# An LSTM scan on one core: tanh of the cell written as a sigmoid, placed ahead of the output gate

## The chip, the core and the metric

The kernel runs on one core of one Trainium2 chip. The time is the device time of the core in microseconds, taken as the median of three runs. A profiled execution of the same program gives the trace.

## What is computed

An LSTM over 1,024 steps with batch 2 and width 256 is added to its input; a modulated linear layer then adds to the result.

```python
def step(carry, xw_t):
    prev_h, prev_c = carry
    a = xw_t + prev_h @ Wh
    i = jax.nn.sigmoid(a[:, :Hdim])
    f = jax.nn.sigmoid(a[:, Hdim:2 * Hdim])
    o = jax.nn.sigmoid(a[:, 2 * Hdim:3 * Hdim])
    g = jnp.tanh(a[:, 3 * Hdim:])
    next_c = f * prev_c + i * g
    next_h = o * jnp.tanh(next_c)
    return ((next_h, next_c), next_h)
...
x = x + _L0_cond_ref(x, cond_1024, L0_cond_Wx, L0_cond_Wh, L0_cond_b)
# the second layer: x * (y / 16), times weight, times rsqrt(sum + EPS)
x = x + _L1_cond_ref(x, cond_1024, L1_cond_weight)
```

All arithmetic is in float32.

## The kernel before

The width of 256 stands as two halves of 128 partitions, j = 0 and 1, and everything in a step is done for the one half and then for the other. The scan is a loop of 256 turns (`NBODY`) with four steps in each (`T`, index s), written out by hand for each engine; the order of each engine's instructions is the order of the code, and semaphores join the engines.

**TensorE** makes the sums. A group, `cell(s, j, n, k)`, is the product for output half j, gate n (in, forget, candidate) and input half k of h: four matmuls on 32 columns of weights and 16 columns of `hst` each (`add_h`, L207 to L211). In the trace each float32 matmul is two records. Twelve groups make the three gates of both halves; the six with k = 0 need only the first half of h, the six with k = 1 the second. A step first waits for `h_ready[0]`, does the three groups of j = 0, k = 0 and then one and a half of j = 1, k = 0 (L243 to L248). Then it waits for `h_ready[1]` (L250), does the three groups of j = 0, k = 1, which ends `sums_ready[0]`, the rest of j = 1, and ends `sums_ready[1]`. After that come the four groups of the output gate (`pS`, `osum_ready[j]`), then work that no step waits for at once: the products of x for the next turn (`pX`, L191, 24 matmuls in s = 0 and 1, 16 in s = 2), and in s = 2 and 3 a matmul on zeros (`filler`, `FILL`, L222).

**ScalarE** (L171 to L182) does for each step: sigmoid of the three gates of half 0, the same of half 1 (L176), then for each half the sigmoid of the output gate (L180, from PSUM) and the tanh of the cell (L182, from SBUF), in this order: o0, t0, o1, t1. o waits for `osum_ready[j]`, t for `cell_ready[j]`. The tanh of the candidate g is made from a sigmoid: its weights are doubled, a constant -0.5 stands beside the gates, and so the cell is kept at half its value.

**VectorE** (L335 to L355) makes the cell of each half by two fused multiply-and-sums with their accumulator reads (L340, `junk` and `gates`), and then for each half h = tanh * o into `hst` (L351), which ends `h_ready[j]`. In the last step of a turn it also carries the sums of x into PSUM (`carry_cells`, L322, and `carry_outs`, L326).

**GpSimd** (L130 to L139) waits for both halves of h of a step and adds them to x in place (L137); after the fourth step it copies the x of the turn after next into `xp` (L123), for which TensorE's `pX` work in the next turn's first step waits (`xp_ready`, L266).

After the loop TensorE does the second layer's matmuls (L281, L290), VectorE scales and adds (L368), and SyncE writes out.

Of the kernel before, what the change touches and what calls it, by code (L numbers as in the profile page):

```python
# [4 lines left out]
P = 128  # L5
# [3 lines left out]
ALU = mybir.AluOpType  # L9


def build(nc, xT_in, condT_in, Wx, Wh, bC, w, outT):
    D, B, SEQ = xT_in.shape
    K = D // P
    G = 4
# [10 lines left out]
    WARM = 26  # L26
    FILL = (0, 0, 1, 1)
    NOUT = 512
# [3 lines left out]
    with ctx:  # L32
# [12 lines left out]
        xp = sb("xp", [P, K, ROWS])  # L45
        hst = sb("hst", [P, K, T * WIDE])
        gates = sb("gates", [P, K, B, CELL])
        junk = sb("junk", [P, K, B, G])
        ogate = sb("ogate", [P, K, B])
        zeros = sb("zeros", [P, P])  # L50
        tanhc = sb("tanhc", [P, K, B])
        warmed = sb("warmed", [P, 1])
# [29 lines left out]
        gates_ready = [sem(f"gates_ready{j}") for j in range(K)]  # L82
        bias_doubled = sem("bias_doubled")
        x_carried = [sem(f"x_carried{n}") for n in range(K + 1)]
        cell_ready = [sem(f"cell_ready{j}") for j in range(K)]
        tanh_ready = [sem(f"tanh_ready{j}") for j in range(K)]
        h_ready = [sem(f"h_ready{j}") for j in range(K)]
# [31 lines left out]
        def _(pool):  # L119
# [10 lines left out]
            def bodies(lo, hi, aside=None):  # L130
                with pool.Fori(lo, hi) as it:
                    for s in range(T):
                        for j in range(K):
                            pool.wait_ge(h_ready[j], it * T + (s + 2))
                        at = h_slot((s + 1) % T)
                        now = xh[:, :, :, bass.ds(it * T + s, 1)]
                        pool.tensor_tensor(now, now, hst[:, :, at:at + B].unsqueeze(3), ALU.add).then_inc(xh_ready, 1)  # L137
                    pool.wait_ge(x_summed, it + 2)
                    spread(bass.ds(it * T + 2 * T, T))  # L139
                    if aside is not None:  # L140
                        aside()
# [20 lines left out]
        def _(act):  # L162
# [8 lines left out]
            with act.Fori(0, NBODY) as it:  # L171
                for s in range(T):
                    cols = slice(B * s, B * (s + 1))
                    for j in range(K):
                        act.wait_ge(sums_ready[j], it * T + (s + 1))
                        act.activation(gates[:, j, :, 0:NG].rearrange("p b n -> p n b"), cells[j][:, :, cols],  # L176
                                       ACT.Sigmoid).then_inc(gates_ready[j], 1)
                    for j in range(K):
                        act.wait_ge(osum_ready[j], it * T + (s + 1))
                        act.activation(ogate[:, j, :], outs[j][:, cols], ACT.Sigmoid)  # L180
                        act.wait_ge(cell_ready[j], it * T + (s + 1))
                        act.activation(tanhc[:, j, :], gates[:, j, :, AT_C], ACT.Tanh, scale=2.0).then_inc(tanh_ready[j], 1)  # L182

# [4 lines left out]
        def _(pe):  # L188
# [49 lines left out]

            early, late = range(G // 2), range(G // 2, G)
            with pe.Fori(0, NBODY) as it:  # L240
                for s in range(T):
# [5 lines left out]
                    cell(s, 1, 0, 0)  # L247
                    cell(s, 1, 1, 0, early)  # L248

# [3 lines left out]
                    last.then_inc(sums_ready[0], 1)  # L253
                    cell(s, 1, 1, 0, late)
                    cell(s, 1, 2, 0)
                    for n in range(NG):
# [38 lines left out]
        def _(dve):  # L295
# [20 lines left out]
            dve.wait_ge(wh_loaded, 16)  # L316
            dve.tensor_scalar(wh_sb[:, :, g_cols], wh_sb[:, :, g_cols], 2.0, None, ALU.mult).then_inc(operands_ready, 1)
            for j in range(K):
                dve.tensor_copy(hst[:, j, h_slot(0):h_slot(0) + B], condT[:, j, :]).then_inc(h_ready[j], 1)

# [14 lines left out]
            with dve.Fori(0, NBODY) as it:  # L335
                for s in range(T):
# [11 lines left out]
                    for j in range(K):  # L348
                        dve.wait_ge(tanh_ready[j], it * T + (s + 1))
                        at = h_slot((s + 1) % T)  # L350
                        dve.tensor_tensor(hst[:, j, at:at + B], tanhc[:, j, :], ogate[:, j, :], ALU.mult).then_inc(h_ready[j], 1)  # L351
                        if s == T - 1 and j == 0:
# [45 lines left out]
```

## Time and profile before

| what | us |
|---|---|
| median of three runs | 1866.57 (1865.84 to 1866.58) |
| the profiled execution's own time | 1865.51 |
| its span, first to last instruction | 1863.7 |
| TensorE busy | 1794.8 (96%) |
| VectorE busy | 916.5 (49%) |
| ScalarE busy | 900.9 (48%) |
| GpSimd busy | 259.2 (14%) |

Busy times are modelled for matmuls, and TensorE's busy time counts records that overlap, so 96% isn't TensorE at its peak. Four steps make a turn of the loop; at 1000 us of the span the first records of the steps stand at 1000.73, 1002.50, 1004.26 and 1006.04 us, 1.77 us apart. Times of rows are in microseconds from the start of the span, and two decimals are what the timeline gives.

### The profile page before, as it was taken

How to read it: one execution, taken by the hardware profiler on the slowest of the kernel's cores; microseconds unless marked ns; L12 is line 12 of the kernel's file. 1: busy time of each engine (PE TensorE's matmuls, PEld its weight loads, DVE VectorE, ACT ScalarE, POOL GpSimd, SP SyncE). 2: the span in 40 equal slices, each digit the busy share in tenths (PEclk: the TensorE clock that was granted, in tenths of full speed). 3: DMA queues.
4: the chain of work that ended last, by engine and by line, in shares of the span. 5: the costliest groups of instructions: out<-in, count | busy, mean ns of one | idle time of the engine just before them, and what ended most of it. 6: DMA issues, size and time to landing. Idle time of an engine off the chain costs nothing.

```text
span 1863.7 us, 358217 instructions
## 1 busy us (share of the span) xinstructions
PE 1794.8 (96%) x165116; PEld 1627.1 (87%) x165116; DVE 916.5 (49%) x11034; ACT 900.9 (48%) x6148; POOL 259.2 (14%) x1293
## 2 busy tenths in 40 slices
PE   7999999999999999999999999999999999999998
PEld 6888888888888888888888888888888888888886
DVE  2454544455445544454444544455444544455444
ACT  2444444444444444444444444444444444444443
POOL 0111111111111111111111111111111111111110
PEclk7999999999999999999999999999999999999999
DMA  3000000000000000000000000000000000000001
GB/s 98 0 0 0 0 0 0 0 0 0 0 0 0 0 0 0 0 0 0 0 0 0 0 0 0 0 0 0 0 0 0 0 0 0 0 0 0 0 0 45
DMA packets 4585, 6.69 MB, mean 4 GB/s; under 512 B 1248, under 2 KB 3040, under 8 KB 4576
## 3 DMA queue, kind: packets, MB, share of 16 engines
q1 hardware_dynamic: 3872, 5.51, 0.9%
q10 hardware_dynamic: 704, 1.05, 0.2%
q8 instruction: 7, 0.11, 0.0%
q14 instruction: 2, 0.02, 0.0%
HBM read 4.46 MB, written 2.10 MB: 4 GB/s over the span
## 4 chain that ended last, share of the span: by engine, by line
PE 85%; DVE 10%; ACT 3%; issue 2%; DMA 0%; SPq 0%; POOL 0%; DVEq 0%
PE pG L209 51%; PE pX L191 17%; PE pS L209 12%; DVE junk L340 6%; PE pF L222 3%; ACT gates L176 3%; DVE hst L351 2%; DVE pG L322 1%; PE pX L290 1%; DVE gates L340 0%; DMA xh<-in_xT_dram 0%; PE pS L281 0%; DVE ores L368 0%; SPq L105 0%; ACT tanhc L182 0%
## 5 line engine op out<-in xcount | busy, mean ns | idle before, releaser
L209 PEld LDWEIGHTS pG<-hst,wh_sb 128*32 128x32 f32 x98304 | 981.1, 111 | 219.1 <-DVE hst L351 172.1
L209 PE MATMUL pG<-hst,wh_sb 128*32 128x16 f32 x98304 | 1081.8, 186 | 60.6 <-DVE hst L351 53.4
L340 DVE CUSTOM_DVE_ANT_1 junk<-gates 128x4 f32<-128x4 f32 x4096 | 506.9, 162 | 824.7 <-ACT gates L176 772.5
L176 ACT ACTIVATE gates<-pG 128x6 f32<-128x6 f32 x2048 | 372.5, 182 | 928.7 <-PE pG L209 782.9
L209 PE MATMUL pS<-hst,wh_sb 128*32 128x16 f32 x32768 | 495.5, 185 | 0.0
L191 PE MATMUL pX<-xp,wx_sb 128*32 128x8 f32 x32896 | 459.3, 181 | 2.8 <-issue 1.8
L137 POOL TENSOR_TENSOR xh<-xh,hst 128x4 f32 (+1 forms) x1024 | 208.6, 204 | 1575.4 <-DVE hst L351 1575.4
L182 ACT ACTIVATE tanhc<-gates 128x2 f32<-128x2 f32 x2048 | 410.5, 200 | 13.5
L209 PEld LDWEIGHTS pS<-hst,wh_sb 128*32 128x32 f32 x32768 | 397.9, 108 | 0.0
L191 PEld LDWEIGHTS pX<-xp,wx_sb 128*32 128x32 f32 x32896 | 391.8, 108 | 3.2 <-issue 1.9
L351 DVE TENSOR_TENSOR hst<-tanhc,ogate 128x2 f32<-128x2 f32 x2048 | 329.7, 161 | 100.4 <-ACT tanhc L182 0.2
L340 DVE DVE_READ_ACCUMULATOR2_ANT gates<- 128x1 f32 x4096 | 339.1, 83 | 0.0
L180 ACT ACTIVATE ogate<-pS 128x2 f32<-128x2 f32 x2048 | 338.9, 170 | 0.3
L222 PE MATMUL pF<-zeros,picks 128*32 128x128 f32 x1076 | 214.0, 285 | 0.0
L322 DVE TENSOR_TENSOR pG<-pX,bias_col 128x24 f32<-128x24 f32 x514 | 95.0, 185 | 1.1 <-PE pX L191 1.1
L222 PEld LDWEIGHTS pF<-zeros,picks 128*32 128x32 f32 x1076 | 77.3, 109 | 0.6
L123 POOL COPY xp<-xh 128x16 f32 (+1 forms) x258 | 51.7, 200 | 10.5 <-DMA xh<-in_xT_dram 9.0
L326 DVE TENSOR_TENSOR pS<-pX,bias_o 128x16 f32<-128x16 f32 x257 | 45.2, 176 | 0.0
L290 PE MATMUL pX<-xh,wmod 128*128 128x512 f32 x32 | 14.0, 595 | 0.0
L290 PEld LDWEIGHTS pX<-xh,wmod 128*128 128x128 f32 x32 | 6.0, 190 | 7.2 <-issue 6.9
L368 DVE SCALAR_TENSOR_TENSOR ores<-pX,demod,xh 128x512 f32<-128x512 f32 x8 | 6.0, 750 | 8.0 <-PE pX L290 8.0
L306 DVE TENSOR_SCALAR yscale<-condT 128x4 f32<-128x4 f32 x1 | 0.2, 169 | 7.5 <-DMA condT<-in_condT_dram 7.5
(30 smaller groups left out, 13.9 us busy)
## 6 DMA issues: line engine op xcount, KB each, us to landing
outT_dram<-ores SPq DMA_DIRECT2D x8, 256.0 KB, 2.5
xh<-in_xT_dram SPq DMA_DIRECT2D x6, 320.0 KB
wh_sb<-in_Wh_dram ACTq DMA_DIRECT2D x1, 1024.0 KB, 8.0
wx_sb<-in_Wx_dram SPq DMA_DIRECT2D x1, 1024.0 KB, 7.4
w_sb<-in_w_dram SPq DMA_DIRECT2D x1, 256.0 KB, 6.9
xh<-in_xT_dram SPq DMA_DIRECT2D x2, 64.0 KB, 7.9
condT<-in_condT_dram ACTq DMA_DIRECT2D x1, 2.0 KB, 7.7
bias_col<-in_bC_dram ACTq DMA_DIRECT2D x1, 3.0 KB, 7.4
```

The source lines that it names most:

```text
L123: pool.tensor_copy(xp[:, :, :].rearrange("p k (t b) -> p k b t", b=B), xh[:, :, :, t]).then_inc(xp_ready, 1)
L137: pool.tensor_tensor(now, now, hst[:, :, at:at + B].unsqueeze(3), ALU.add).then_inc(xh_ready, 1)
L176: act.activation(gates[:, j, :, 0:NG].rearrange("p b n -> p n b"), cells[j][:, :, cols], ACT.Sigmoid).then_inc(gates_ready[j], 1)
L180: act.activation(ogate[:, j, :], outs[j][:, cols], ACT.Sigmoid)
L182: act.activation(tanhc[:, j, :], gates[:, j, :, AT_C], ACT.Tanh, scale=2.0).then_inc(tanh_ready[j], 1)
L191: last = pe.matmul(to[c * Q:(c + 1) * Q, :], tile(wx_sb[:, k, :], c, j, g), xp[:, k, :], start=(k == 0), stop=(k == K - 1), skip_group_che ...
L209: last = pe.matmul(to[c * Q:(c + 1) * Q, :], tile(wh_sb[:, k, :], c, j, g), hst[:, k, WIDE * t:WIDE * (t + 1)], start=False, stop=True, sk ...
L222: pe.matmul(pF[0:Q, 0:P], picks[:, :], zeros[:, :], start=start, stop=True, skip_group_check=True)
L322: dve.tensor_tensor(cells[j][:, :, 0:ROWS], xcells[j], bias_col[:, j, :].unsqueeze(2).broadcast_to([P, NG, ROWS]), ALU.add).then_inc(x_car ...
L326: dve.tensor_tensor(pS[:, :, 0:ROWS], xouts, bias_o[:, :].unsqueeze(2).broadcast_to([P, K, ROWS]), ALU.add).then_inc(x_carried[K], 1)
L340: cell = dve.tensor_tensor_reduce(out=junk[:, j, b, :], in0=gates[:, j, b, AT_I:AT_F + 1].unsqueeze(2).broadcast_to([P, 2, 2]), in1=gates[ ...
L351: dve.tensor_tensor(hst[:, j, at:at + B], tanhc[:, j, :], ogate[:, j, :], ALU.mult).then_inc(h_ready[j], 1)
```

## The change

The tanh of the cell becomes a sigmoid of four times the halved cell, `sigc` (tanh(c) = 2 sigmoid(2c) - 1). VectorE's h becomes (sigc - 0.5) * o, which is half of h. The weights `wh_sb` are doubled for it (the candidate's times four in all), and the first h is halved. On ScalarE the order in each step becomes t0, o0, t1, o1, and h of a half waits for its o (`factors_ready[j]`). GpSimd doubles the halved h into a new buffer, `whole`, waits for that and adds it to x: two instructions where there was one. TensorE does one group of j = 1, k = 0 ahead of the wait for the second half of h in place of one and a half, and the matmul on zeros of the fourth step is gone.

```diff
-    FILL = (0, 0, 1, 1)
+    FILL = (0, 0, 1, 0)
...
-                        pool.tensor_tensor(now, now, hst[:, :, at:at + B].unsqueeze(3), ALU.add).then_inc(xh_ready, 1)
+                        pool.tensor_tensor(whole[:, s, :, :], hst[:, :, at:at + B], hst[:, :, at:at + B], ALU.add).then_inc(whole_ready, 1)
+                        pool.wait_ge(whole_ready, it * T + (s + 1))
+                        pool.tensor_tensor(now, now, whole[:, s, :, :].unsqueeze(3), ALU.add).then_inc(xh_ready, 1)
...
                     for j in range(K):
+                        act.wait_ge(cell_ready[j], it * T + (s + 1))
+                        act.activation(sigc[:, j, :], gates[:, j, :, AT_C], ACT.Sigmoid, scale=4.0)
                         act.wait_ge(osum_ready[j], it * T + (s + 1))
-                        act.activation(ogate[:, j, :], outs[j][:, cols], ACT.Sigmoid)
-                        act.wait_ge(cell_ready[j], it * T + (s + 1))
-                        act.activation(tanhc[:, j, :], gates[:, j, :, AT_C], ACT.Tanh, scale=2.0).then_inc(tanh_ready[j], 1)
+                        act.activation(ogate[:, j, :], outs[j][:, cols], ACT.Sigmoid).then_inc(factors_ready[j], 1)
...
-            early, late = range(G // 2), range(G // 2, G)
...
                     cell(s, 1, 0, 0)
-                    cell(s, 1, 1, 0, early)
 
                     pe.wait_ge(h_ready[1], it * T + (s + 1))
                     for n in range(NG):
                         last = cell(s, 0, n, 1)
                     last.then_inc(sums_ready[0], 1)
-                    cell(s, 1, 1, 0, late)
-                    cell(s, 1, 2, 0)
+                    for n in range(1, NG):
+                        cell(s, 1, n, 0)
...
-            dve.tensor_scalar(wh_sb[:, :, g_cols], wh_sb[:, :, g_cols], 2.0, None, ALU.mult).then_inc(operands_ready, 1)
+            ifo_cols = slice(0, (O_ + 1) * D)
+            dve.tensor_scalar(wh_sb[:, :, ifo_cols], wh_sb[:, :, ifo_cols], 2.0, None, ALU.mult)
+            dve.tensor_scalar(wh_sb[:, :, g_cols], wh_sb[:, :, g_cols], 4.0, None, ALU.mult).then_inc(operands_ready, 1)
...
-                        dve.tensor_tensor(hst[:, j, at:at + B], tanhc[:, j, :], ogate[:, j, :], ALU.mult).then_inc(h_ready[j], 1)
+                        dve.scalar_tensor_tensor(out=hst[:, j, at:at + B], in0=sigc[:, j, :], scalar=-0.5, in1=ogate[:, j, :],
+                                                 op0=ALU.add, op1=ALU.mult).then_inc(h_ready[j], 1)
```

On ScalarE, in each step, the rows before the change (the numbers behind the names are the halves):

```order
L176 ACTIVATE gates<-pG 128x3x2 [waits sums_ready0]
L176 ACTIVATE gates<-pG 128x3x2 [waits sums_ready1]
L180 ACTIVATE ogate<-pS 128x2 [waits osum_ready0]
L182 ACTIVATE tanhc<-gates 128x2 [waits cell_ready0]
L180 ACTIVATE ogate<-pS 128x2 [waits osum_ready1]
L182 ACTIVATE tanhc<-gates 128x2 [waits cell_ready1]
```

And with it:

```order
L179 ACTIVATE gates<-pG 128x3x2 [waits sums_ready0]
L179 ACTIVATE gates<-pG 128x3x2 [waits sums_ready1]
L183 ACTIVATE sigc<-gates 128x2 [waits cell_ready0]
L185 ACTIVATE ogate<-pS 128x2 [waits osum_ready0]
L183 ACTIVATE sigc<-gates 128x2 [waits cell_ready1]
L185 ACTIVATE ogate<-pS 128x2 [waits osum_ready1]
```

The output gate's sigmoid moved from ahead of the cell's function to behind it, in both halves.

On TensorE, in the third step of a turn (s = 2), the rows before:

```order
L209 MATMUL pG<-hst,wh_sb 32x16 [waits h_ready0]
L209 MATMUL pG<-hst,wh_sb 32x16 x17
L209 MATMUL pG<-hst,wh_sb 32x16 [waits h_ready1]
L209 MATMUL pG<-hst,wh_sb 32x16 x29
L209 MATMUL pS<-hst,wh_sb 32x16 x16
```

And with the change:

```order
L212 MATMUL pG<-hst,wh_sb 32x16 [waits h_ready0]
L212 MATMUL pG<-hst,wh_sb 32x16 x15
L212 MATMUL pG<-hst,wh_sb 32x16 [waits h_ready1]
L212 MATMUL pG<-hst,wh_sb 32x16 x31
L212 MATMUL pS<-hst,wh_sb 32x16 x16
```

Two matmuls moved from ahead of the wait for the second half of h to behind it: 16 ahead and 32 behind, where there were 18 and 30.

## Rows read from the trace of the kernel before

**Rows 1.** The page: busy time by engine, and the chain that ended last

```profile
PE 1794.8 (96%) x165116; PEld 1627.1 (87%) x165116; DVE 916.5 (49%) x11034; ACT 900.9 (48%) x6148; POOL 259.2 (14%) x1293
...
PE 85%; DVE 10%; ACT 3%; issue 2%; DMA 0%; SPq 0%; POOL 0%; DVEq 0%
```

**Rows 2.** View of waits: who waited for whom, us, times, longest

```profile
PEld pG L209 <- DVE hst L351: 172.1, 513, 0.5
```

**Rows 3.** Timeline, weight loads of one step: start, length, engine, line, operation

```profile
1002.50 0.93 PEld L209 LDWEIGHTS pG<-hst,wh_sb 128*32 128x32 f32 x95
...
1003.62 0.41 PEld L191 LDWEIGHTS pX<-xp,wx_sb 128*32 128x32 f32 x32
...
1004.26 0.44 PEld L209 LDWEIGHTS pG<-hst,wh_sb 128*32 128x32 f32 x40 [0.20 <-DVE hst L351]
```

**Rows 4.** Timeline, ScalarE in the same step; last row: the second L176

```profile
1003.27 0.51 ACT L176 ACTIVATE gates<-pG 128x6 f32<-128x6 f32 x2 [0.74 <-PE pG L209]
1003.75 0.17 ACT L180 ACTIVATE ogate<-pS 128x2 f32<-128x2 f32 x1
1003.82 0.20 ACT L182 ACTIVATE tanhc<-gates 128x2 f32<-128x2 f32 x1
1003.92 0.17 ACT L180 ACTIVATE ogate<-pS 128x2 f32<-128x2 f32 x1
1004.10 0.20 ACT L182 ACTIVATE tanhc<-gates 128x2 f32<-128x2 f32 x1
...
1003.60 0.18 ACT L176 ACTIVATE gates<-pG 128x6 f32<-128x6 f32 x1
```

**Rows 5.** Timeline, VectorE in the same step

```profile
1003.66 0.08 DVE L340 DVE_READ_ACCUMULATOR2_ANT gates<- 128x1 f32 x1
...
1003.98 0.08 DVE L340 DVE_READ_ACCUMULATOR2_ANT gates<- 128x1 f32 x1
1004.05 0.16 DVE L351 TENSOR_TENSOR hst<-tanhc,ogate 128x2 f32<-128x2 f32 x1
...
1004.34 0.16 DVE L351 TENSOR_TENSOR hst<-tanhc,ogate 128x2 f32<-128x2 f32 x1
```

**Rows 6.** Busy by stretch, instructions on hst: matmuls, then loads, counts in brackets

```profile
1004.26:1004.50 0.24, 0.23 (x28) 0.23 (x32) 0.16 (x1) 0.00 (x0) 1.00 0.00 0
```

**Rows 7.** Groups by line and shape: total, mean ns, idle before

```profile
L351 DVE TENSOR_TENSOR hst<-tanhc,ogate 128x2 f32<-128x2 f32 x2048 | 329.7, 161 | 100.4 <-ACT tanhc L182 0.2
...
L169 ACT ACTIVATE warmed<-zeros 128x1 f32<-128x1 f32 x1 | 0.2, 203 | 0.0
...
L306 DVE TENSOR_SCALAR yscale<-condT 128x4 f32<-128x4 f32 x1 | 0.2, 169 | 7.5 <-DMA condT<-in_condT_dram 7.5
```

**Rows 8.** Timeline, GpSimd after the fourth step of a turn

```profile
1006.50 0.20 POOL L137 TENSOR_TENSOR xh<-xh,hst 128x4 f32 x1 [1.57 <-DVE hst L351]
1006.68 0.20 POOL L123 COPY xp<-xh 128x16 f32 x1
```

**Rows 9.** Timeline, weight loads of the step that follows

```profile
1006.04 0.94 PEld L209 LDWEIGHTS pG<-hst,wh_sb 128*32 128x32 f32 x95 [0.48 <-DVE hst L351]
...
1007.19 0.54 PEld L191 LDWEIGHTS pX<-xp,wx_sb 128*32 128x32 f32 x48
```

**Rows 10.** Timeline, all engines before the loop

```profile
10.00 0.42 DVE L317 TENSOR_SCALAR wh_sb<-wh_sb 128x512 f32<-128x512 f32 x1
...
11.67 0.28 DVE L322 TENSOR_TENSOR pG<-pX,bias_col 128x24 f32<-128x24 f32 x2 [1.10 <-PE pX L191]
```

**Rows 11.** Busy time by stretch, all engines, with the granted clock

```profile
core 0: us, PE busy (x) PEld busy (x) DVE busy (x) ACT busy (x) POOL busy (x), PEclk, DMA share, GB/s
12.20:30.70 18.50, 10.62 (x644) 9.67 (x644) 3.29 (x41) 3.41 (x24) 0.61 (x3) 0.50 0.02 5
...
33.00:52.00 19.00, 18.58 (x1722) 17.01 (x1716) 8.93 (x107) 8.75 (x60) 2.61 (x13) 1.00 0.38 117
1000.00:1007.09 7.09, 6.88 (x668) 6.26 (x658) 3.55 (x44) 3.51 (x24) 0.99 (x5) 1.00 0.00 0
```

More of the change, by code:

```diff
@@ L46, in build @@
         hst = sb("hst", [P, K, T * WIDE])
+        whole = sb("whole", [P, T, K, B])
         gates = sb("gates", [P, K, B, CELL])
@@ L50, in build @@
         zeros = sb("zeros", [P, P])
-        tanhc = sb("tanhc", [P, K, B])
+        sigc = sb("sigc", [P, K, B])
         warmed = sb("warmed", [P, 1])
@@ L82, in build @@
         gates_ready = [sem(f"gates_ready{j}") for j in range(K)]
-        bias_doubled = sem("bias_doubled")
+        bias_doubled, whole_ready = sem("bias_doubled"), sem("whole_ready")
         x_carried = [sem(f"x_carried{n}") for n in range(K + 1)]
         cell_ready = [sem(f"cell_ready{j}") for j in range(K)]
-        tanh_ready = [sem(f"tanh_ready{j}") for j in range(K)]
+        factors_ready = [sem(f"factors_ready{j}") for j in range(K)]
         h_ready = [sem(f"h_ready{j}") for j in range(K)]
@@ L316, in _ @@
             dve.wait_ge(wh_loaded, 16)
-            dve.tensor_scalar(wh_sb[:, :, g_cols], wh_sb[:, :, g_cols], 2.0, None, ALU.mult).then_inc(operands_ready, 1)
+            ifo_cols = slice(0, (O_ + 1) * D)
+            dve.tensor_scalar(wh_sb[:, :, ifo_cols], wh_sb[:, :, ifo_cols], 2.0, None, ALU.mult)
+            dve.tensor_scalar(wh_sb[:, :, g_cols], wh_sb[:, :, g_cols], 4.0, None, ALU.mult).then_inc(operands_ready, 1)
             for j in range(K):
-                dve.tensor_copy(hst[:, j, h_slot(0):h_slot(0) + B], condT[:, j, :]).then_inc(h_ready[j], 1)
+                dve.tensor_scalar(hst[:, j, h_slot(0):h_slot(0) + B], condT[:, j, :], 0.5, None, ALU.mult).then_inc(h_ready[j], 1)
             def carry_cells(j):
@@ L348, in _ @@
                     for j in range(K):
-                        dve.wait_ge(tanh_ready[j], it * T + (s + 1))
+                        dve.wait_ge(factors_ready[j], it * T + (s + 1))
                         at = h_slot((s + 1) % T)
-                        dve.tensor_tensor(hst[:, j, at:at + B], tanhc[:, j, :], ogate[:, j, :], ALU.mult).then_inc(h_ready[j], 1)
+                        dve.scalar_tensor_tensor(out=hst[:, j, at:at + B], in0=sigc[:, j, :], scalar=-0.5, in1=ogate[:, j, :],
+                                                 op0=ALU.add, op1=ALU.mult).then_inc(h_ready[j], 1)
                         if s == T - 1 and j == 0:
```

## The prediction

> **What bounds the kernel now.** I read the page first. TensorE is busy 96% of the span, but the chain that ended last also has 10% on VectorE and 3% on ScalarE [rows 1]: TensorE is not alone in setting the pace. The view of waits says the same: the weight loads of the next step waited for VectorE's h 513 times, 172 us in all [rows 2]. So I went to one step in the timeline, the third of a turn. Its weight loads start at 1002.50 and the next step's at 1004.26 [rows 3], 1.77 us apart (rounding aside), and 1,024 steps of 1.77 us are 1,812 of the span's 1863.7 us. All that follows is about that 1.77.
>
> Each step has two loops, one through each half of h. The first half ends at 4.05 + 0.16 = 1004.21 [rows 5], and the loads begin at 1004.26 [rows 3]: TensorE stood waiting and started 0.05 later. So the first half sets the step. The second half ends at 4.34 + 0.16 = 1004.50 [rows 5]; with the same 0.05 TensorE may use it from 1004.55. Does it come in time? 95 loads start within 0.93 less the last one's own 0.11, so 0.0087 us apart [rows 3]; the four and a half groups ahead of the wait are 18 matmuls or 36 records, 0.31 us, and end at 1004.57. The second half is early by about 0.03 us. That is the whole slack, and three edits draw on it.
>
> **The second half's loop, before.** From one end of the second h to the next: 0.05 to TensorE's restart. From there to ScalarE's second gates: the records behind the wait start at 1002.50 + 0.31 = 1002.81, the second L176 at 1003.60 [rows 4], so 0.79. From that to the end of the second cell at 3.98 + 0.08 = 1004.06 [rows 5]: 0.46. To the tanh at 1004.10: 0.04; the tanh: 0.20 [rows 4]. To the product at 1004.34: 0.04; the product: 0.16 [rows 5]. Sum 1.74, which is the 1.77 less the slack of 0.03.
>
> **Four groups, not four and a half.** Two matmuls, 4 records, move behind the wait: 4 x 0.0087 = +0.035 in this loop. For the first half it is a gain: its sums can end 0.035 sooner, if the second h is there.
>
> **The output gate behind the cell's function.** Before, the second half's o had been done long ahead (1003.92 to 1004.09) while the cell was still being made, and only the tanh lay on the path. Now h waits for o, and o stands in ScalarE's queue behind a function that itself waits for the cell. Nothing hides it. How soon may o start behind the other? Two pairs in the rows: o to tanh 3.75 to 3.82, 0.07; tanh to o 3.82 to 3.92, 0.10 [rows 4]. The second has the new order, and I take 0.10. Then the new piece is 0.10 + 0.17 for o, 0.27 in place of 0.20: +0.07. Bounds: with 0.07 it is +0.04. The function itself costs the same: a sigmoid read from SBUF took 203 ns, near the tanh's 0.20 [rows 7], and only its distance to o counts.
>
> The Trainium skill (ScalarE: Activation LUTs, What ACT_TABLE_LOAD costs) says that back-to-back ACTIVATEs overlap by about 93 ns. By it o would start 0.20 - 0.09 = 0.11 behind, and this estimate would add 10 us to the result below; the trace's pairs are a little closer, and the sum goes by them.
>
> **VectorE's product.** The new form has a constant ahead of the product. No row has it in this size; the product takes 161 ns, an operation with a constant on four elements 169 [rows 7]. A gain has no ground: it does one operation more on the same operands. Between 0 and +0.01; I take +0.005.
>
> **TensorE after a real stop.** Now TensorE will stand at the second wait, and resume with its queue full. In the first 0.24 us after a stop 32 loads start but 28 matmuls [rows 6]: 0.0075 and 0.0086 apart, against 0.0087 on average. Over the first 32 records that is between 0 and -0.04; I take -0.02.
>
> **The sum.** 1.74 + 0.035 + 0.07 + 0.005 - 0.02 = 1.83 us for the second half's loop. It is over 1.77, so the slack is gone and this loop becomes the pace: TensorE reaches the wait 32 x 0.0087 = 0.28 after a step's start and the second h comes about 0.08 later, in every step. The first half's own loop would be shorter: its tanh had waited for o (1003.82, where the cell was ready at 3.66 + 0.08 = 1003.74 and 0.04 more is the usual start [rows 4, 5]), so 1.77 - 0.035 - 0.04 + 0.07 = 1.765. It can't run by itself, since its sums are ended behind the same wait. 0.06 us x 1,024 = +61 us on the profiled execution's 1865.51; the median of the runs lies 1 us above it, so 1866.57 + 61 = 1928.
>
> **What lies beside.** GpSimd: two instructions and a wait in place of one. Alone it waits for nothing critical, except in a turn's first step, where its copy of x releases `pX`. Before: the second h ends 2.00 after the fourth step's start [rows 5], at 1006.26; GpSimd adds from 6.50 and its copy ends at 6.68 + 0.20 = 1006.88 [rows 8], 0.31 before `pX` starts at 1007.19 [rows 9]. New: the added instruction costs its 0.20 and a wait for its own result, between 0 and the 0.24 that GpSimd took from the h to its start: +0.20 to +0.44, and the second h comes 0.08 later in the step, as `pX` does. So the copy is late by 0.13 at most. `pX` is the last work of that step; its loads take 0.54 and end at 1007.73, 0.08 before the next at 1007.81 (1006.04 + 1.77) [rows 9], and the longer step adds 0.06 to that. In the worst case nothing is left, and 0 is taken; a wait longer by 0.1 would cost 256 x 0.1 = 26 us.
>
> The matmul on zeros of the fourth step: TensorE stood still afterwards anyway, so it is worth nothing by itself. SyncE's queue isn't touched. Before the loop the scaling of `wh_sb` takes 2,048 in place of 512 elements in each partition: at most 3 x 0.42 = 1.26 us more, where VectorE stood idle 1.10 until 11.67 [rows 10], so 0 to 0.2 us; I take 0. After the loop one more GpSimd instruction, hidden by the first matmuls: 0.
>
> **Rivals.** (A) No loss, or a gain: the two functions go through ScalarE almost side by side, both being of one kind now. The second half's loop is 1.83 with 0.10 between their starts; with 0.04 it is 1.77 and nothing changes, which is the point from which it decides, and with 0.02 it is 1.75: 20 us less, 1846. For it: before, the pairs were of two kinds, a sigmoid and a tanh, and no row shows two sigmoids at that distance. Against: both orders of the mixed pair are at 0.07 and 0.10, and at 0.07 the result is still 1.80, or 1897. Chance 0.07.
>
> (B) GpSimd's copy holds `pX` and through it the next step, as worked out: 1928 + 26 = 1954. For it: 0.24 from h to start shows how slow its waits are. Against: it needs all of the worst case and more. Chance 0.08.
>
> (C) The granted clock falls. Between 12.2 and 30.7 us it was at 0.50, the 1.2 GHz level, with 35 load records a us and steps of some 4.6 us; from 33 us on it was at 1.00 with 90 a us, and 93 in the turn at 1000 us [rows 11]. The new turn has 2 load records less in 7.32 us in place of 7.09, so 90 a us again. If it fell all the same, each 20 steps at that pace would cost 57 us: over 1985. Chance 0.04.
>
> **How the numbers follow.** The forecast (a step of 1.79 to 1.86) gets 0.81. Its bounds: with o at 0.07 and the full 0.04 gained after a stop 1.78, which is 1877; without that gain, with 0.01 for the product, 1.855, which is 1954. I give 1888 to 1966, which takes in (B) and leaves out (A), (C) and the last corner of the lower bounds. A measurement of this kernel can tell 0.2%, 4 us. Faster by more than that: 0.04, slower: 0.92, the same: 0.04.
>
> **What would show it.** In the profile after, the steps lie 1.83 apart; within a step TensorE's loads break after 32 records for about 0.08 us, and the view of waits has TensorE waiting for h twice a step, so over 1,000 times more often. On ScalarE o starts 0.10 behind the cell's function and the product 0.04 behind o's end. If the loads don't break, (A) holds; if `pX` waits for `xp`, (B); if PEclk has a digit under 9 after the first slice, (C). I am wrong if o starts closer than 0.04 to the function ahead of it.

## The result, and the profile after the change

The changed kernel takes 1921.65 us (median of 4 runs, 1920.77 to 1922.18), the kernel before beside it 1866.21 us: a ratio of 1.0298, 95% interval 1.0285 to 1.0311. It is 55.4 us slower; 1928 was predicted, with 1888 to 1966 as the range. The profiled execution took 1921.88 us, its span is 1920.1.

The page after, busy time by engine and the chain that ended last, as in [rows 1]:

```profile
PE 1787.3 (93%) x164604; PEld 1662.8 (87%) x164604; DVE 926.6 (48%) x11035; ACT 885.9 (46%) x6148; POOL 459.7 (24%) x2317
...
PE 84%; DVE 10%; ACT 3%; issue 2%; DMA 0%; SPq 0%; POOL 0%; ACTq 0%; DVEq 0%
```

The chain has hardly changed its shares: it still goes through TensorE for the most part, and the page alone wouldn't say where the time went. The timeline of one step does. The weight loads of the third step of a turn and of the one behind it, as in [rows 3]:

```profile
1004.25 1.01 PEld L212 LDWEIGHTS pG<-hst,wh_sb 128*32 128x32 f32 x95
...
1006.08 0.23 PEld L212 LDWEIGHTS pG<-hst,wh_sb 128*32 128x32 f32 x17 [0.18 <-DVE hst L354]
```

The steps lie 1.83 us apart, where it was 1.77 [rows 3]. The same 95 loads take 1.01 from first start to last end, where it was 0.93: something stands in the middle of them. The view by stretch counts the loads in the first 0.24 and the first 0.35 us of that step (columns: stretch, its length, busy time of the loads and their count, granted clock, DMA):

```profile
1004.25:1004.49 0.24, 0.24 (x32) 1.00 0.00 0
1004.25:1004.60 0.35, 0.34 (x32) 1.00 0.00 0
```

And for the same 0.35 us from a step's start in the kernel before:

```profile
1004.26:1004.61 0.35, 0.34 (x41) 1.00 0.00 0
```

After the change, 32 loads have started by 0.24 us, the 16 matmuls ahead of the wait, and not one more by 0.35. Before, TensorE went on without a break. The missing loads are those behind the wait for the second half of h. ScalarE in that step, as in [rows 4]:

```profile
1005.06 0.18 ACT L179 ACTIVATE gates<-pG 128x6 f32<-128x6 f32 x1 [0.70 <-PE pG L212]
1005.42 0.18 ACT L179 ACTIVATE gates<-pG 128x6 f32<-128x6 f32 x1 [0.18 <-PE pG L212]
1005.56 0.20 ACT L183 ACTIVATE sigc<-gates 128x2 f32<-128x2 f32 x1
1005.67 0.15 ACT L185 ACTIVATE ogate<-pS 128x2 f32<-128x2 f32 x1
1005.92 0.20 ACT L183 ACTIVATE sigc<-gates 128x2 f32<-128x2 f32 x1
1006.03 0.15 ACT L185 ACTIVATE ogate<-pS 128x2 f32<-128x2 f32 x1
```

And VectorE, as in [rows 5], from the h of the step before to the second h of this one:

```profile
1004.39 0.16 DVE L354 SCALAR_TENSOR_TENSOR hst<-sigc,ogate 128x2 f32<-128x2 f32 x1 [0.20 <-ACT ogate L185]
...
1005.81 0.08 DVE L343 DVE_READ_ACCUMULATOR2_ANT gates<- 128x1 f32 x1
1005.86 0.16 DVE L354 SCALAR_TENSOR_TENSOR hst<-sigc,ogate 128x2 f32<-128x2 f32 x1
1006.22 0.16 DVE L354 SCALAR_TENSOR_TENSOR hst<-sigc,ogate 128x2 f32<-128x2 f32 x1 [0.20 <-ACT ogate L185]
```

The second cell ends at 1005.89, its sigmoid starts at 1005.92, the gate at 1006.03 and ends at 1006.18, and only then, at 1006.22, comes the second h. It ends at 1006.38, 1.83 after the one before (1004.39 + 0.16 = 1004.55). So the loop through the second half goes round in 1.83 us, and TensorE stands at its wait in nearly every step.

The costs by group, as in [rows 7]:

```profile
L183 ACT ACTIVATE sigc<-gates 128x2 f32<-128x2 f32 x2048 | 418.4, 204 | 89.9 <-DVE gates L343 2.5
...
L354 DVE SCALAR_TENSOR_TENSOR hst<-sigc,ogate 128x2 f32<-128x2 f32 x2048 | 328.8, 161 | 169.9 <-ACT ogate L185 143.4
...
L185 ACT ACTIVATE ogate<-pS 128x2 f32<-128x2 f32 x2048 | 314.5, 154 | 0.1
```

The cell's function is 204 ns as a sigmoid and the new product 161 ns, what the plain one took: neither has a price. The gate itself takes 154 ns. VectorE's idle time ahead of the product grew from 100.4 [rows 7] to 169.9 us, and 143.4 us of it is put down to the gate; the view names a releaser for the longer gaps alone, so the 0.2 us of [rows 7] doesn't mean that VectorE hardly waited for ScalarE before.

### The profile page after: what moved, and what is told of

Read it like the earlier page. It is cut to its first block, busy times and chain, and to the rows that moved or that the text cites. A ratio compares the mean times of both kernels' runs of the same rounds, so it can differ in the third digit from the quotient of the medians.

```text
span 1920.1 us, 358468 instructions
## 1 busy us (share of the span) xinstructions
PE 1787.3 (93%) x164604; PEld 1662.8 (87%) x164604; DVE 926.6 (48%) x11035; ACT 885.9 (46%) x6148; POOL 459.7 (24%) x2317
## 4 chain that ended last, share of the span: by engine, by line
PE 84%; DVE 10%; ACT 3%; issue 2%; DMA 0%; SPq 0%; POOL 0%; ACTq 0%; DVEq 0%
PE pG L212 52%; PE pX L194 17%; PE pS L212 11%; DVE junk L343 7%; PE pF L225 3%; ACT gates L179 3%; DVE hst L354 2%; DVE pG L325 1%; PE pX L291 1%; DVE gates L343 0%; DMA xh<-in_xT_dram 0%; ACT sigc L183 0%; PE pS L282 0%; DVE ores L372 0%; SPq L106 0%
## 5 line engine op out<-in xcount | busy, mean ns | idle before, releaser
L212 PE MATMUL pG<-hst,wh_sb 128*32 128x16 f32 x98304 | 1142.6, 186 | 123.8 <-DVE hst L354 115.1
L212 PEld LDWEIGHTS pG<-hst,wh_sb 128*32 128x32 f32 x98304 | 1036.7, 111 | 239.4 <-DVE hst L354 186.3
L138 POOL TENSOR_TENSOR whole<-hst 128x4 f32<-128x4 f32 x1024 | 203.7, 199 | 1250.6 <-DVE hst L354 1250.6
L212 PE MATMUL pS<-hst,wh_sb 128*32 128x16 f32 x32768 | 479.8, 185 | 0.0
L183 ACT ACTIVATE sigc<-gates 128x2 f32<-128x2 f32 x2048 | 418.4, 204 | 89.9 <-DVE gates L343 2.5
L354 DVE SCALAR_TENSOR_TENSOR hst<-sigc,ogate 128x2 f32<-128x2 f32 x2048 | 328.8, 161 | 169.9 <-ACT ogate L185 143.4
L185 ACT ACTIVATE ogate<-pS 128x2 f32<-128x2 f32 x2048 | 314.5, 154 | 0.1
L140 POOL TENSOR_TENSOR xh<-xh,whole 128x4 f32 (+1 forms) x1024 | 205.2, 200 | 181.1 <-POOL whole L138 179.2
L225 PE MATMUL pF<-zeros,picks 128*32 128x128 f32 x564 | 110.6, 286 | 0.0
L225 PEld LDWEIGHTS pF<-zeros,picks 128*32 128x32 f32 x564 | 41.7, 110 | 0.4
```

Of the source, the lines that this page charges most:

```text
L138: pool.tensor_tensor(whole[:, s, :, :], hst[:, :, at:at + B], hst[:, :, at:at + B], ALU.add).then_inc(whole_ready, 1)
L140: pool.tensor_tensor(now, now, whole[:, s, :, :].unsqueeze(3), ALU.add).then_inc(xh_ready, 1)
L183: act.activation(sigc[:, j, :], gates[:, j, :, AT_C], ACT.Sigmoid, scale=4.0)
L212: last = pe.matmul(to[c * Q:(c + 1) * Q, :], tile(wh_sb[:, k, :], c, j, g), hst[:, k, WIDE * t:WIDE * (t + 1)], start=False, stop=True, sk ...
L225: pe.matmul(pF[0:Q, 0:P], picks[:, :], zeros[:, :], start=start, stop=True, skip_group_check=True)
L354: dve.scalar_tensor_tensor(out=hst[:, j, at:at + B], in0=sigc[:, j, :], scalar=-0.5, in1=ogate[:, j, :], op0=ALU.add, op1=ALU.mult).then_i ...
```

## The experiments

The theory: a step has two loops, one through each half of h, and the change made the second half's the longer one, by the output gate's 0.06 us behind the cell's function and by the 0.035 us of two more matmuls behind the wait. The rivals: GpSimd's two instructions, the sigmoid form, and the missing matmul on zeros.

The times, with the ratio to runs of the kernel before made beside them (1865.94, 1866.46 and 1865.99 us):

| run | what it is | us | ratio to before, 95% interval |
|---|---|---|---|
| a_o_first | changed, ScalarE's order put back | 1863.28 | 0.9975 to 0.9994 |
| a_18_ahead | changed, 18 matmuls ahead of the wait | 1898.01 | 1.0157 to 1.0191 |
| a_20_ahead | changed, 20 ahead | 1899.19 | 1.0164 to 1.0198 |
| a_14_ahead | changed, 14 ahead | 1954.99 | 1.0462 to 1.0497 |
| a_pool_once | changed, one GpSimd instruction; it leaves out the doubling, so its output has half of h in it | 1920.94 | 1.0277 to 1.0311 |
| a_fill | changed, matmul on zeros put back | 1923.31 | 1.0289 to 1.0323 |
| b_o_behind | before, gate behind the tanh | 1913.90 | 1.0240 to 1.0274 |
| b_16_ahead | before, 16 ahead | 1863.07 | 0.9973 to 0.9992 |
| b_form | before, with the sigmoid form alone | 1868.13 | 1.0004 to 1.0022 |
| b_o_behind_nofill | b_o_behind, no matmul on zeros in the fourth step | 1893.95 | 1.0136 to 1.0167 |
| b_best17 | before, another order and 17 ahead | 1883.03 | 1.0076 to 1.0106 |
| b_best17_nofill | the same, no matmul on zeros there | 1882.44 | 1.0074 to 1.0102 |

**a_o_first: the order of ScalarE put back**

```diff
-                    for j in range(K):
-                        act.wait_ge(cell_ready[j], it * T + (s + 1))
-                        act.activation(sigc[:, j, :], gates[:, j, :, AT_C], ACT.Sigmoid, scale=4.0)
-                        act.wait_ge(osum_ready[j], it * T + (s + 1))
-                        act.activation(ogate[:, j, :], outs[j][:, cols], ACT.Sigmoid).then_inc(factors_ready[j], 1)
+                    act.wait_ge(osum_ready[0], it * T + (s + 1))
+                    act.activation(ogate[:, 0, :], outs[0][:, cols], ACT.Sigmoid)
+                    act.wait_ge(cell_ready[0], it * T + (s + 1))
+                    act.activation(sigc[:, 0, :], gates[:, 0, :, AT_C], ACT.Sigmoid, scale=4.0).then_inc(factors_ready[0], 1)
+                    act.wait_ge(osum_ready[1], it * T + (s + 1))
+                    act.activation(ogate[:, 1, :], outs[1][:, cols], ACT.Sigmoid)
+                    act.wait_ge(cell_ready[1], it * T + (s + 1))
+                    act.activation(sigc[:, 1, :], gates[:, 1, :, AT_C], ACT.Sigmoid, scale=4.0).then_inc(factors_ready[1], 1)
```

> The changed kernel with ScalarE's order put back: output gate, cell's function, for each half. Theory (the second half's loop through h is the pace, and the output gate behind the cell's function is most of what it gained): the loop falls by the 0.26 us from the function's start to the gate's end less the function's 0.20, so by 0.06 from 1.83 to 1.77, where the first half's loop, whose function again waits for the gate, takes over: 1860 to 1867 us. Rival (GpSimd's doubling, the sigmoid form or the missing matmul on zeros cost the time): 1915 or more.

Measured 1863.28. Everything else of the change is still in it, and it is 58 us faster than the changed kernel and 2.7 faster than the one before. So without the new order nothing is left of the loss. That doesn't make the order all of it: the next two runs and a_18_ahead below show what the two matmuls take beside it.

**b_16_ahead, b_o_behind: each part of the change alone, in the kernel before**

b_16_ahead is the change's edit on TensorE:

```diff
-                    cell(s, 1, 1, 0, early)
...
-                    cell(s, 1, 1, 0, late)
+                    cell(s, 1, 1, 0, range(0, G))
                     cell(s, 1, 2, 0)
```

> The kernel before, with nothing changed but 16 matmuls ahead of the second h in place of 18. Theory: the second half's loop goes from 1.745 by 0.035 to 1.78 less up to 0.02, the first half's stays at 1.77, since its tanh waits for the output gate's sums, which are not moved: 0 to 8 us more, 1866 to 1874. Rival (the two parts of the change cost by themselves what they cost together): 20 us more.

Measured 1863.07: no cost, a gain of 3.4 us, on the other side of what I had expected. Its steps are 1.771 us in the trace where the kernel before has 1.769, so the gain is not in them; the section on the turn's start below has what it may be. So the two matmuls cost nothing by themselves, while the second half's loop has slack; with the new order they cost 24 us (1898.01 with 18 ahead, 1921.65 with 16).

b_o_behind is the change's order on ScalarE, with tanh:

```diff
-                    for j in range(K):
-                        act.wait_ge(osum_ready[j], it * T + (s + 1))
-                        act.activation(ogate[:, j, :], outs[j][:, cols], ACT.Sigmoid)
-                        act.wait_ge(cell_ready[j], it * T + (s + 1))
-                        act.activation(tanhc[:, j, :], gates[:, j, :, AT_C], ACT.Tanh, scale=2.0).then_inc(tanh_ready[j], 1)
+                    act.wait_ge(cell_ready[0], it * T + (s + 1))
+                    act.activation(tanhc[:, 0, :], gates[:, 0, :, AT_C], ACT.Tanh, scale=2.0)
+                    act.wait_ge(osum_ready[0], it * T + (s + 1))
+                    act.activation(ogate[:, 0, :], outs[0][:, cols], ACT.Sigmoid).then_inc(tanh_ready[0], 1)
+                    act.wait_ge(cell_ready[1], it * T + (s + 1))
+                    act.activation(tanhc[:, 1, :], gates[:, 1, :, AT_C], ACT.Tanh, scale=2.0)
+                    act.wait_ge(osum_ready[1], it * T + (s + 1))
+                    act.activation(ogate[:, 1, :], outs[1][:, cols], ACT.Sigmoid).then_inc(tanh_ready[1], 1)
```

> The kernel before, with nothing changed but ScalarE's order: tanh, output gate, for each half, and h waits for the gate. Theory: the second half's loop goes from 1.745 by 0.06 to 1.80, its slack of 0.025 is spent and 0.035 are left, less what TensorE gains after a stop: 20 to 36 us more, 1886 to 1902, as much as the changed kernel with 18 matmuls ahead. Rival (a sigmoid behind a sigmoid costs more than behind a tanh, or the rest of the change has a price): clearly below that kernel.

Measured 1913.90, 12 us over the range. Three of its four steps are 1.79 to 1.80 us, as the theory has it. The turn's first step is 1.92, with a stop of TensorE near its start that the theory doesn't have (below). In the other three steps the theory holds: with the gate in the same place and a tanh ahead of it, the gate starts 0.11 behind and the steps are those of a_18_ahead.

**b_form: what is left of the change**

The edits of a_o_first, and with them:

```diff
-    FILL = (0, 0, 1, 0)
+    FILL = (0, 0, 1, 1)
...
                     cell(s, 1, 0, 0)
+                    cell(s, 1, 1, 0, range(2))
...
-                    for n in range(1, NG):
-                        cell(s, 1, n, 0)
+                    cell(s, 1, 1, 0, range(2, G))
+                    cell(s, 1, 2, 0)
```

> The changed kernel with ScalarE's order, the 18 matmuls ahead and the matmul on zeros of the kernel before: what is left of the change is the sigmoid form, h halved, the product with a constant and GpSimd's two instructions. Theory: the form costs nothing, since a sigmoid takes the tanh's 204 ns and the new product the old one's 161: 1864 to 1869 us. Rival (the form has a price of its own): 5 us more or above.

Measured 1868.13, 2.1 us above the kernel beside it and within what was expected. By the interval, the sigmoid form, the halved h and GpSimd's doubling cost 1 to 4 us together.

**a_14_ahead, a_18_ahead, a_20_ahead: how many matmuls stand ahead of the wait**

a_18_ahead:

```diff
                     cell(s, 1, 0, 0)
+                    cell(s, 1, 1, 0, range(2))
...
-                    for n in range(1, NG):
-                        cell(s, 1, n, 0)
+                    cell(s, 1, 1, 0, range(2, G))
+                    cell(s, 1, 2, 0)
```

a_20_ahead:

```diff
                     cell(s, 1, 0, 0)
+                    cell(s, 1, 1, 0, range(4))
...
-                    for n in range(1, NG):
-                        cell(s, 1, n, 0)
+                    cell(s, 1, 2, 0)
```

a_14_ahead:

```diff
-                    cell(s, 1, 0, 0)
+                    cell(s, 1, 0, 0, range(2))
...
                     last.then_inc(sums_ready[0], 1)
+                    cell(s, 1, 0, 0, range(2, G))
```

> The changed kernel with three and a half groups (14 matmuls) ahead of the second h. Theory: two more matmuls in the second half's loop, 0.035 us a step, 36 us more: 1957. Rival (the wait is hidden or TensorE makes it up after a stop): under 1940.

> The changed kernel with four and a half groups (18 matmuls) ahead of the second h, as before the change. Theory: 4 records of 0.0087 us leave the second half's loop, 1.83 becomes 1.795, and the first half's own loop (0.31 to the wait and 1.47 from there) is at 1.78 just under it: 36 us less, 1886. Rival (the wait for the second h is not what paces): within 5 us of 1921.6.

> The changed kernel with five groups (20 matmuls) ahead of the second h. Theory of two loops: the second half's falls to 1.76, but the first half's sums now end later, 0.345 us to the wait and 1.47 from there, 1.815: 1907 us, so slower than with 18 though faster than with 16. Rival (only the second half's loop counts): a further 36 us less, 1850.

With 14, 16, 18 and 20 ahead: 1954.99, 1921.65, 1898.01, 1899.19. The first difference is 33 us for two matmuls, 0.033 us a step, against 0.035 forecast. From 18 to 20 nothing more is gained, though two more matmuls leave the second half's loop: the other loop has taken over. It is a little shorter than the expectation for 20 had it, 1.804 in place of 1.815 us, and so the time lies 8 us under the forecast of 1907. The starts of the weight loads in a turn of a_20_ahead show it:

```profile
1044.89 0.91 PEld L212 LDWEIGHTS pG<-hst,wh_sb 128*32 128x32 f32 x96 [0.60 <-DVE hst L354]
...
1046.69 0.91 PEld L212 LDWEIGHTS pG<-hst,wh_sb 128*32 128x32 f32 x96
...
1048.50 0.91 PEld L212 LDWEIGHTS pG<-hst,wh_sb 128*32 128x32 f32 x96
```

The loads take 0.91, with no stop among them, and the steps are 1.80 and 1.81 apart: TensorE waits for the first h alone. In a_18_ahead the steps should be 1.795:

```profile
1045.40 0.94 PEld L212 LDWEIGHTS pG<-hst,wh_sb 128*32 128x32 f32 x95 [0.57 <-DVE hst L355]
...
1047.23 0.93 PEld L212 LDWEIGHTS pG<-hst,wh_sb 128*32 128x32 f32 x95
...
1049.02 0.94 PEld L212 LDWEIGHTS pG<-hst,wh_sb 128*32 128x32 f32 x95
...
1050.82 0.94 PEld L212 LDWEIGHTS pG<-hst,wh_sb 128*32 128x32 f32 x95 [0.21 <-DVE hst L355]
```

Three are (1.79, 1.80, 1.79), and the first of the turn is 1.83. The 12 us by which it missed the forecast are for the most part that 0.035 to 0.04 in each of 256 turns, 9 to 10 us. The next section has what it probably is.

**a_pool_once, a_fill: the rivals taken away**

a_pool_once:

```diff
-                        pool.tensor_tensor(whole[:, s, :, :], hst[:, :, at:at + B], hst[:, :, at:at + B], ALU.add).then_inc(whole_ready, 1)
-                        pool.wait_ge(whole_ready, it * T + (s + 1))
-                        pool.tensor_tensor(now, now, whole[:, s, :, :].unsqueeze(3), ALU.add).then_inc(xh_ready, 1)
+                        pool.tensor_tensor(now, now, hst[:, :, at:at + B].unsqueeze(3), ALU.add).then_inc(xh_ready, 1)
```

a_fill:

```diff
-    FILL = (0, 0, 1, 0)
+    FILL = (0, 0, 1, 1)
```

> The changed kernel with one GpSimd instruction a step, as before the change: it adds the halved h to x, so the doubling is left out and the output holds half of h. In the profile after the change the first cell instruction of a turn's first step takes 198 ns in place of 165 while GpSimd copies x, and that step is 1.863 us long, but the next is 1.796. Theory: the delay is in the first half alone, which is not the pace, and is given back a step later: 1919 to 1922 us, with four steps of 1.83. Rival (GpSimd's second instruction costs part of the 55 us): 8 us less or more.

> The changed kernel with the matmul on zeros in the fourth step put back. Theory: TensorE stands idle there anyway and the clock is at 1.00 with or without: 1920 to 1923 us. Rival (idle TensorE costs clock or a slower restart): 5 us less or more.

Measured 1920.94 and 1923.31 (0.3 over its range): neither is where the 55 us went. But GpSimd does do something. In the changed kernel, the copy of x on GpSimd, and VectorE's first two cell instructions of a turn's first step:

```profile
1060.18 0.20 POOL L124 COPY xp<-xh 128x16 f32 x1
```

```profile
1060.20 0.20 DVE L343 CUSTOM_DVE_ANT_1 junk<-gates 128x4 f32<-128x4 f32 x1 [0.63 <-ACT gates L179]
1060.33 0.08 DVE L343 DVE_READ_ACCUMULATOR2_ANT gates<- 128x1 f32 x1
```

One step later the same instruction takes 0.17, and its read starts 0.09 behind in place of 0.13:

```profile
1062.03 0.17 DVE L343 CUSTOM_DVE_ANT_1 junk<-gates 128x4 f32<-128x4 f32 x1 [0.72 <-ACT gates L179]
1062.12 0.08 DVE L343 DVE_READ_ACCUMULATOR2_ANT gates<- 128x1 f32 x1
```

GpSimd's second instruction moved its copy into VectorE's work, and there VectorE took 0.03 us more: in all of 241 turns of the changed kernel the copy lies over this instruction, which takes 0.205 us on the mean; in a_pool_once the copy ends 0.11 before it and it takes 0.168. But that both run at once isn't enough. In a_20_ahead the copy lies over it too, and it takes its usual time:

```profile
1045.84 0.20 POOL L124 COPY xp<-xh 128x16 f32 x1
```

```profile
1045.89 0.16 DVE L343 CUSTOM_DVE_ANT_1 junk<-gates 128x4 f32<-128x4 f32 x1 [0.67 <-ACT gates L179]
```

It is slower in the kernels whose copy starts 0.02 to 0.04 us ahead of it on the mean (the changed one, a_fill, a_14_ahead, a_18_ahead, a_o_first), and not in the two where that is 0.07 and 0.08 (a_20_ahead, b_form). What the two contend for stays open.

What became of that 0.03 in the changed kernel, in the starts of the loads of the same turn:

```profile
1059.17 1.01 PEld L212 LDWEIGHTS pG<-hst,wh_sb 128*32 128x32 f32 x95 [0.54 <-DVE hst L354]
...
1061.03 0.97 PEld L212 LDWEIGHTS pG<-hst,wh_sb 128*32 128x32 f32 x95
...
1062.83 1.01 PEld L212 LDWEIGHTS pG<-hst,wh_sb 128*32 128x32 f32 x95
```

The steps are 1.86 and 1.80, which is twice 1.83. The delay hit the first half, whose loop isn't the pace: TensorE started 0.03 later and then stood 0.04 less at the second wait (0.97 for the loads in place of 1.01). In a_pool_once the step starts are at 1057.43, 1059.26, 1061.09 and 1062.92, 1.83 each, and the total is the same to 0.7 us. In a_18_ahead, where both loops are about as long, the same delay isn't given back: 1.83 and then 1.79. No run took the copy away there, but b_o_behind_nofill (next) comes near: it has the same order and 18 ahead, without GpSimd's second instruction, and its turn's first step is 1.81 where no other stop falls in it.

**b_o_behind_nofill: the stop at the turn's start**

```diff
-    FILL = (0, 0, 1, 1)
+    FILL = (0, 0, 1, 0)
```

> The kernel before with the output gate behind the tanh, as in the run b_o_behind, and without the matmul on zeros of the fourth step. In b_o_behind every turn's first step stopped for 0.09 us after its first 12 records (in the kernel before 50 of 225 turns did), which no theory of the loops through h explains. If the stop hangs on how late TensorE comes to the loop's branch, it goes with that matmul, and the time falls to that of the changed kernel with 18 ahead: 1894 to 1899 us. If it hangs on something else: 1910 or more.

Measured 1893.95, 20 us less than b_o_behind and just under the expected 1894 to 1899. The loads in the first 0.16 us of a turn, with the stop (b_o_behind) and in a turn without it (b_o_behind_nofill):

```profile
1053.64 0.26 PEld L212 LDWEIGHTS pG<-hst,wh_sb 128*32 128x32 f32 x10 [0.50 <-DVE hst L354]
```

```profile
1035.65 0.27 PEld L212 LDWEIGHTS pG<-hst,wh_sb 128*32 128x32 f32 x22 [0.57 <-DVE hst L354]
```

TensorE starts a turn with nine loads and then starts none for some 0.10 us, though h is there (the tenth of the first row is the one behind the stop). In the trace of b_o_behind every turn behind the first 20 does so. In the kernel before it is 52 of the last 241 turns, and there the turn's first step is 1.90 in place of 1.78, as between these two:

```profile
998.83 1.05 PEld L209 LDWEIGHTS pG<-hst,wh_sb 128*32 128x32 f32 x95 [0.48 <-DVE hst L351]
...
1000.73 0.18 PEld L209 LDWEIGHTS pG<-hst,wh_sb 128*32 128x32 f32 x11
```

Without the matmul on zeros the stop is rarer, and it isn't gone: 69 of 241 turns of b_o_behind_nofill have it, for the most part every third one, with 0.07 to 0.08 us between two loads. Their first step is 1.89 in place of 1.81. One of them, beside the turn at 1035.65 above, whose loads take 0.94:

```profile
1042.85 1.02 PEld L212 LDWEIGHTS pG<-hst,wh_sb 128*32 128x32 f32 x95 [0.57 <-DVE hst L354]
```

In the kernel before, too, the stops come in a rhythm, in every fourth or fifth turn. In the changed kernel 31 of 241 turns have one, and it costs them next to nothing: their first step is 1.877 us on the mean against 1.871, since the stop ends before the second h comes, for which TensorE waits anyway. In b_16_ahead it is 40 turns, and they cost 0.09: 3.8 us over all 256 turns, against 6.6 in the kernel before, which is about the size of its gain of 3.4. The matmul on zeros in front of the branch doesn't bring the stop in every kernel: with it, a_fill stops in about a quarter of its turns, and b_best17 below in none. In the kernel before, the branch comes 0.03 us later in the turns that stop, but in a_fill and a_14_ahead turns with the branch at the same time do both. What makes the stop stays open. What is shown is that b_o_behind loses 20 us to it against the same kernel without that matmul.

**b_best17, b_best17_nofill: a version meant to beat both**

If the second half's gate must not stand behind the cell's function, but the first half's tanh needn't wait for its gate, the order is tanh 0, gate 0, gate 1, tanh 1:

```diff
-                    for j in range(K):
-                        act.wait_ge(osum_ready[j], it * T + (s + 1))
-                        act.activation(ogate[:, j, :], outs[j][:, cols], ACT.Sigmoid)
-                        act.wait_ge(cell_ready[j], it * T + (s + 1))
-                        act.activation(tanhc[:, j, :], gates[:, j, :, AT_C], ACT.Tanh, scale=2.0).then_inc(tanh_ready[j], 1)
+                    act.wait_ge(cell_ready[0], it * T + (s + 1))
+                    act.activation(tanhc[:, 0, :], gates[:, 0, :, AT_C], ACT.Tanh, scale=2.0)
+                    act.wait_ge(osum_ready[0], it * T + (s + 1))
+                    act.activation(ogate[:, 0, :], outs[0][:, cols], ACT.Sigmoid).then_inc(tanh_ready[0], 1)
+                    act.wait_ge(osum_ready[1], it * T + (s + 1))
+                    act.activation(ogate[:, 1, :], outs[1][:, cols], ACT.Sigmoid)
+                    act.wait_ge(cell_ready[1], it * T + (s + 1))
+                    act.activation(tanhc[:, 1, :], gates[:, 1, :, AT_C], ACT.Tanh, scale=2.0).then_inc(tanh_ready[1], 1)
...
-                    cell(s, 1, 1, 0, early)
+                    cell(s, 1, 1, 0, range(1))
...
-                    cell(s, 1, 1, 0, late)
+                    cell(s, 1, 1, 0, range(1, G))
```

> The kernel before (tanh, whole h) with ScalarE in the order tanh 0, gate 0, gate 1, tanh 1 and 17 matmuls ahead of the second h. Theory of two loops: the first half's no longer waits for the gate's sums and is 0.293 + 1.471 = 1.764; the second half's keeps its gate off the path and is 1.745 + 0.017 = 1.76, both under 1.77: 4 to 7 us less than before, 1860. Rival (the gate's place matters for both halves): 1866 or more.

> The same without the matmul on zeros of the fourth step. Theory: the same step of 1.764; the stops at a turn's start cost 3 to 7 us in the kernels with a step of 1.77, and this shows whether they are fewer without it: 1857 to 1861 us. Rival (that matmul keeps the pace up): above the kernel with it.

Measured 1883.03 and 1882.44, over 20 us worse than expected. They are 17 us above the kernel before, and the two don't differ. A step of b_best17 in the trace, its first loads and the next step's, and what ScalarE does:

```profile
1037.95 0.95 PEld L212 LDWEIGHTS pG<-hst,wh_sb 128*32 128x32 f32 x95
...
1039.74 0.95 PEld L212 LDWEIGHTS pG<-hst,wh_sb 128*32 128x32 f32 x95
```

```profile
1038.73 0.18 ACT L176 ACTIVATE gates<-pG 128x6 f32<-128x6 f32 x1 [0.74 <-PE pG L212]
1039.07 0.18 ACT L176 ACTIVATE gates<-pG 128x6 f32<-128x6 f32 x1 [0.16 <-PE pG L212]
1039.23 0.20 ACT L179 ACTIVATE tanhc<-gates 128x2 f32<-128x2 f32 x1
1039.34 0.15 ACT L181 ACTIVATE ogate<-pS 128x2 f32<-128x2 f32 x1
1039.39 0.17 ACT L183 ACTIVATE ogate<-pS 128x2 f32<-128x2 f32 x1
```

The first sums are done 0.78 us after the step's start, as with 18 matmuls ahead (0.77, [rows 3, 4]), and the second at 1.12, later than with 18 (1.10). In b_16_ahead they stand at 0.74 and 1.10 (a step from 1038.13, gates at 1038.87 and 1039.23). The expectation took each matmul as 0.017 us wherever it stands. The first and the second gates are both 0.016 later than a straight line between 16 and 18 would put them, so cutting a group of four behind its first matmul costs about what one more matmul would. The first matmul of a group and the first one behind the wait go to the same quarter of the array's columns; whether that is the reason wasn't tried. The other 0.006 of the 0.023 by which the step (1.787) missed 1.764 lies in the 1.471 from the wait to the next step, which was read in the changed kernel. It isn't the same in every kernel: in a_20_ahead it is 1.456. Why stays open.

Against the kernel before, the loss has a plainer reason. The first gates stand at the same 0.77 to 0.78 in both, and from there to the next step it is 0.99 before (1003.27 to 1004.26, [rows 3, 4]) and 1.01 here (1038.73 to 1039.74); over the third steps of 241 turns the medians are 0.996 and 1.014. The 0.018 between them, 1,024 times, are 18 us. It is the order in the first half: its tanh starts sooner, but its gate now ends later than the tanh did (1.54 behind the step's start, where the tanh ended at 1.52). The prediction had this trade in its sum for the first half's own loop, 0.04 less and 0.07 more, and the design of this version passed over it. So tanh 0 ahead of gate 0 loses by itself. With 16 ahead the order wasn't run; the second half's loop is 1.77 there already, so by the loops it would gain nothing.

## Why the prediction was right, point by point

- **Where the time goes.** The second half's loop became the pace, as the sum had it. The forecast gave it 1.83 us, the trace has 1.829. The stop after 32 records is there: in the third and fourth step of every turn about 0.12 us between two starts, in the first and second a little less, and in some twenty of the last 963 steps hardly any.
- **The gate behind the cell's function.** The sum took 0.10 to the gate's start and 0.17 for it; it is 0.11 and 0.15, together 0.26 where 0.27 stood. The rule of the Trainium skill (ScalarE: Activation LUTs, What ACT_TABLE_LOAD costs), an overlap of some 93 ns, gives the 0.11 to the hundredth: 204 less 93. For other pairs it is a little short: the pairs of [rows 4] overlap by 0.10. The tanh of the pair that the sum went by had itself stood behind a gate in ScalarE's queue; the functions that had waited for their cell, in the changed kernel and in b_o_behind, have 0.11. Rival (A), a shorter distance between two of one kind, is out: here two sigmoids are 0.11 apart, as tanh and sigmoid are in b_o_behind, and the steps behind the turn's first are those of a_18_ahead.
- **Two matmuls behind the wait.** 0.035 forecast; 0.033 between 14 and 16.
- **The product.** +0.005 forecast, 161 ns against 161: nothing.
- **After a stop.** -0.02 forecast. From 0.05 behind the second h's end, 1004.60, to the second gates at 1005.42 it is 0.82; before it was 0.79, and two matmuls are 0.035 of it. Within the hundredth it is between 0 and -0.01. This term, the gate's and the product's were each off by 0.005 to 0.015, and not all the same way; that they add up to 1.83 to the hundredth is partly luck.
- **From the step to the whole.** Here the sum is off, by 6 us. 0.060 x 1,024 is 61 us, and 55.4 were measured. The sum multiplied one step of the third kind, and passed over what the turn's first step had besides: about 55 stops of 0.12 us, 6.6 us, which the new wait covers. They were in the trace of before. What else differs at the turn's start is smaller: the turn's first two steps of the changed kernel are 3.67 in place of twice 1.829, 3 us over all turns the other way.
- **GpSimd, rival (B).** Its wait for its own result took 0.18 (of 0 to 0.24), and `pX` was not held. That its copy would run into VectorE's work wasn't foreseen; it cost next to nothing here, for the reason above.
- **The clock, rival (C).** 1.00 in the loop: no.
- **What would show it.** The break in the loads is there, and it is 0.12 us between two starts rather than 0.08: the 32 loads ahead of it start within 0.24 us, as [rows 6] had it, where the prediction took 0.28. One sign was wrong. I said the view of waits would have TensorE waiting for h twice as often, over 1,000 times more. It has:

```profile
PEld pG L212 <- DVE hst L354: 186.3, 516, 0.5
```

516 waits where there were 513 [rows 2]. A load lasts 0.11 us and the next starts 0.12 after the last one's start, so the engine hardly looks idle. The waits that now set the pace add next to nothing to the view of waits; the counts by stretch have them.

## What to carry to other kernels

A recurrence that is cut in halves has a loop through each half; write both down, from the end of one h to the next, before moving anything, because what shortens one may lengthen the other, and only the longer one counts. An operation that is ready early belongs ahead of the one that comes last on an in-order engine. Here that held in both halves: even in the first, whose tanh was held up 0.04 us by its gate, the other order was 0.02 slower (b_best17). A delay in the shorter loop is given back a step later, and that is a way to see which loop is the longer.

## What the runs showed of the hardware

- ScalarE: a gate read from PSUM starts 0.11 us behind a function read from SBUF that took 204 ns, with tanh as with sigmoid ahead; behind one on PSUM it is 0.05 (1039.34 to 1039.39 above).
- VectorE's cell instruction took 0.20 us in place of 0.17 where GpSimd's copy of a tile in SBUF had started 0.02 to 0.04 us ahead of it; where the copy had started 0.07 us ahead, in a_20_ahead, it took its 0.16 in spite of it. In a_pool_once, where the copy is over by then, the steps of the turn shown were 1.83 each.
- TensorE starts nine loads behind the loop's branch and then none for 0.07 to 0.11 us, in some turns, in all or in none, though what it waits for is there: 20 us of the time between b_o_behind and b_o_behind_nofill.
- A stop of TensorE about as long as one weight load (0.11 us) hardly shows as a wait: 516 waits against 513, with such a stop in nearly every step.
